# Both mixtures of experts by rows sorted on the chip, in phases, in place of every expert on every row

## The reference

```python
x = L0_attn_x                                  # (16, 256, 128) f32
xn = layernorm(x)
s = L0_attn(xn)                                # linear attention, 16 heads of 64
h = xn + small_causal_attention(rmsnorm(xn))   # 16 heads of 8
h2 = rmsnorm(h)
topw, topi = top_k(softmax(h2 @ gate_w.T), 2)  # weights made to sum to 1
for e in range(8):                             # F = 256
    g = silu(h2 @ w1[e].T) * (h2 @ w3[e].T)
    out += (g @ w2[e].T) * wfull[:, e:e + 1]   # 0 but for the two chosen
x = x + s * silu(h + out)
xn = layernorm(x)
s = L1_attn(xn)                                # chunked gated linear attention, then an FFN of 512
top1 = argmax(xn @ Wg + bg)
y = relu(xn @ W1[e] + b1[e]) @ W2[e] + b2[e]   # H = 512, all e; the chosen one is kept
x = x + s * silu(y[top1])
```

## Time and profile before

| | |
|---|---|
| median of 3 runs | 2884.62 us |
| the profiled execution: its time, its span | 2885.05 us, 2883.3 us |
| busy: TensorE, VectorE, ScalarE, GpSimd | 2600.4, 1507.1, 1542.9, 77.0 us |
| TensorE's mean granted clock | 0.932 of full speed |
| moved by DMA | 85.37 MB, 30 GB/s on the mean |

### The profile page before, as it was taken

How to read it: one execution, slowest core, us unless ns; L and a number is a source line. 1 busy time by engine, 2 the same in 40 slices (tenths; PEclk the granted TensorE clock), 3 DMA queues, 4 the chain that set the end, 5 groups by cost and what they waited for, 6 DMA issues and landing times.

```text
span 2883.3 us, 54394 instructions
## 1 busy us (share of the span) xinstructions
PE 2600.4 (90%) x21120; PEld 1952.1 (68%) x21120; DVE 1507.1 (52%) x3781; ACT 1542.9 (54%) x2721; POOL 77.0 (3%) x40
## 2 busy tenths in 40 slices
PE   4789998999989899998998999899998999999987
PEld 3457767676776767757676676767766677676757
DVE  4355645455554555545455554656546456554543
ACT  1536475463745637375464745637466373744753
POOL 0000000000000000000000000000000000000000
PEclk9789989999999999989999998999989999998998
DMA  3000000100000000000100001000000000001011
GB/s 148 1 32 1 30 34 17 48 1 30 34 31 34 9 23 34 31 33 9 48 9 31 34 24 41 2 30 34 31 34 9 25 32 31 34 16 46 1 61 33
DMA packets 31411, 85.37 MB, mean 30 GB/s; under 512 B 4127, under 2 KB 13351, under 8 KB 30632
## 3 DMA queue, kind: packets, MB, share of 16 engines
q1 hardware_dynamic: 31144, 81.64, 8.2%
HBM read 79.53 MB, written 2.10 MB: 28 GB/s over the span
## 4 chain that ended last, share of the span: by engine, by line
PE 72%; DVE 10%; ACT 8%; issue 8%; SPq 1%; DVEq 0%; DMA 0%; ACTq 0%
PE psum L488 7%; PE psum L495 7%; PE psum L690 4%; PE psum L550 4%; PE psum L468 3%; PE psum L650 3%; PE psum L794 3%; PE psum L520 3%; PE psum L637 2%; PE psum L538 2%; PE psum L741 2%; PE psum L621 2%; PE psum L475 2%; PE psum L577 2%; PE psum L558 2%
## 5 line engine op out<-in xcount | busy, mean ns | idle before, releaser
L894 ACT ACTIVATE gbuf<-psum,cols 128x256 f32<-128x256 f32 x512 | 201.8, 473 | 598.4 <-PE psum L495 582.2
L488 PE MATMUL psum<-x1T_s,ew 128*128 128x256 f32 x1024 | 270.2, 413 | 21.5 <-issue 21.5
L495 PEld LDWEIGHTS psum<-ew,gbuf 128*128 128x128 f32 x2048 | 254.2, 197 | 15.8 <-ACT gbuf L894 9.2
L495 PE MATMUL psum<-ew,gbuf 128*128 128x128 f32 x2048 | 257.2, 280 | 4.1 <-ACT gbuf L894 4.1
L488 PEld LDWEIGHTS psum<-x1T_s,ew 128*128 128x128 f32 x1024 | 200.7, 205 | 87.2 <-issue 61.3
L1156 DVE SCALAR_TENSOR_TENSOR acc<-psum,small,acc 128x128 f32<-128x128 f32 x256 | 77.9, 346 | 335.4 <-PE psum L495 335.4
L468 PE MATMUL psum<-hT_s,w13T 128*128 128x256 f32 x1024 | 243.4, 384 | 0.0
L468 PEld LDWEIGHTS psum<-hT_s,w13T 128*128 128x128 f32 x1024 | 191.6, 192 | 43.7 <-issue 22.1
L880 ACT ACT_TABLE_LOAD x144 | 184.8, 1283 | 2.5
L876 ACT ACT_TABLE_LOAD x128 | 164.2, 1283 | 2.2 <-PE psum L468 0.6
L1131 DVE TENSOR_TENSOR gbuf<-gbuf,psum 128x512 f32<-128x512 f32 x128 | 87.7, 685 | 145.1 <-ACT gbuf L876 145.1
(11 more groups left out here) (212 smaller groups left out, 4828.6 us busy)
## 6 DMA issues: line engine op xcount, KB each, us to landing
ew<-in_ew SPq DMA_DIRECT2D x128, 512.0 KB, 3.6
x<-in_x SPq DMA_DIRECT2D x16, 128.0 KB, 2.1
w13T<-in_w13T SPq DMA_DIRECT2D x1, 2048.0 KB
lqkvg<-in_lqkvg SPq DMA_DIRECT2D x1, 2048.0 KB
out<-y SPq DMA_DIRECT2D x16, 128.0 KB, 1.9
wqkv<-in_wqkv SPq DMA_DIRECT2D x1, 1536.0 KB, 6.5
w2T<-in_w2T SPq DMA_DIRECT2D x1, 1024.0 KB
wrope<-in_wrope SPq DMA_DIRECT2D x1, 640.0 KB, 7.5
```

The costliest lines, as they stand in the source:

```text
L488: last = mm(bank(f"h{e}{j}")[:, a * N:(a + 1) * N], ew[:, e % EB, c * P:(c + 1) * P], x1T[:, :], start=True, stop=True)
L495: last = mm(bank(f"yy{e - 1}")[:, t * P:(t + 1) * P], r1[:, c, t * P:(t + 1) * P], ew[:, (e - 1) % EB, F1 + c * D:F1 + (c + 1) * D], start ...
L894: ins = af(r1[:, c, :], bank(f"h{e}{j}")[:, a * N:(a + 1) * N], ACT.Relu, bias=cols[:, 8 + 4 * e + c:9 + 4 * e + c])
```

## The change

The mixtures are computed for the chosen rows alone. A stage G or a part of C gives each token a slot in a region of its expert in memory (`rows0` and `rows1`, one for each half of 8 batch rows): the token's rank among the same expert's tokens comes from five small products with a triangle of ones (`rank`), a running count is kept in `cnt`. GpSimd scatters the rows there with an indirect DMA. After 8 batch rows VectorE makes a table on one partition (`table`, 14 small operations): for each of 40 tiles of 128 slots (24 are used by the second mixture) its place and its expert. SyncE reads place and expert into registers and loads a tile's weights (384 KB, or 578 KB) and its rows. `tile_step(u)` then does one tile in three steps, each a step behind the one before: transpose, hidden layer, output. SyncE stores a tile's output to `outs0` or `outs1`, and GpSimd gathers each token's two rows (or one) back by the slots, when the row's next stage begins.

As the rows of 8 batch rows must be there before any tile of theirs, the program runs in phases, and what a later stage needs of a row (attention, x2, weights, slots) goes to memory and back (`keepA`, `keepC`):

| segment | times | holds |
|---|---|---|
| H | 1 | the norm of row 0 |
| AH, AHG | 1, 8 | first attention, next row's norm; G: slots and scatter of the row before |
| AHGB | 6 | the same with 5 tiles of the first mixture (first half) |
| AGB, GB | 1, 1 | the last first attention, then tiles and slots alone |
| CB | 8 | second attention of the first half, 5 tiles of the first mixture (second half) |
| CD | 8 | second attention of the second half, 3 tiles of the second mixture (first half) |
| DE | 8 | 3 tiles (second half), outputs of the first half |
| E | 8 | outputs of the second half |

Silu and the last gate of the first mixture are built as Exp, Ln(1 + .), Exp (`logistic`), so that no table is loaded in A and B. The next row's norm (`head`) now stands at the end of the first attention, between `x2` and `h2` on VectorE; `norms1` at the start of the second, behind the gathers. The choice of the second mixture moves ahead of the chunk products' multiply on VectorE. Buffers `w13T`, `w2T` and `ew` go. In the first eight AHG bodies SyncE fills the four regions with zeros (33.5 MB).

```diff
-SEGMENTS = [("AB", 1), ("ABC", 1), ("ABCD", B - 2), ("CD", 1), ("D", 1)]
+HB = B // 2
+CAP = HB * N
+NTB, TB = 40, 5
+NTD, TD = 24, 3
+SEGMENTS = [("H", 1), ("AH", 1), ("AHG", HB), ("AHGB", HB - 2), ("AGB", 1), ("GB", 1), ("CB", HB), ("CD", HB), ("DE", HB), ("E", HB)]
...
+            def tile_loads(stage, count, weights, view):
...
+                for s in range(count):
+                    sp.wait_ge(*given(f"tile{s}_out"))
...
+                    where = sp.value_load(tab[0:1, which, bass.ds(j, 1)], min_val=0, max_val=ROWS // P - 1)
+                    expert = sp.value_load(tab[0:1, which, bass.ds(j + NTB, 1)], min_val=0, max_val=E - 1)
+                    places.append(where)
+                    sp.dma_start(view[:, s, :], weights[expert]).then_inc(sem(f"tile{s}_loaded"), 16)
+                    sp.dma_start(tx[:, s, :], XR[table].rearrange("(j p) d -> j p d", p=P)[where]).then_inc(sem(f"tile{s}_loaded"), 16)
...
+            def attention1():
+
+                g.wait_ge(*given("inA_free"))
...
+                g.dma_start(inA[:, :], KA[row("C")]).then_inc(sem("inA_ready"), 16)
+                g.dma_start(xC[:, :, :], A["x"][row("C")].rearrange("(t p) d -> p t d", p=P)).then_inc(sem("inA_ready"), 16)
+                g.wait_ge(*given("inA_ready", 1, 32))
...
+                        nc.gpsimd.indirect_dma_start(yg[:, k, t, :], None, YR[half("C")], bass.IndirectOffsetOnAxis(ap=slots_in[:, c:c + 1], axis=0)).then_inc(sem("yg_ready"), 16)
                 g.wait_ge(*given("cd_ready"))
...
+                g.wait_ge(*given("slots1_ready"))
...
+                    nc.gpsimd.indirect_dma_start(XR[half("C")], bass.IndirectOffsetOnAxis(ap=slotsC[:, t:t + 1], axis=0), xn1[:, t, :], None).then_inc(sem("scattered1"), 16)
+                g.wait_ge(*given("scattered1", 1, 32))
...
+            def tile_step(u):
...
+                if u < count:
+                    pe.wait_ge(*given(f"tile{u}_loaded", 1, 32))
+                    pe.wait_ge(*emptied(f"tx{u}"))
+                    tr(bank(f"tx{u}")[:, 0:P], tx[:, u, :]).then_inc(*fills(f"tx{u}"))
+                if 1 <= u <= count:
...
+                    for c in range(4):
+                        last = mm(bank(f"th{s}")[:, c * P:(c + 1) * P], view[:, s, c * P:(c + 1) * P], txT[:, s, :], start=True, stop=True)
+                    last.then_inc(*fills(f"th{s}"))
+                if 2 <= u <= count + 1:
...
+                    parts, hidden, w2 = (2, gB, wB) if "B" in stages else (4, rD, wD)
+                    for c in range(parts):
+                        last = mm(bank(f"ty{s}")[:, 0:D], hidden[:, s, c, :], w2[:, s, 4 * P + c * D:4 * P + (c + 1) * D], start=(c == 0), stop=(c == parts - 1))
...
+            def logistic(dst, src, ready):
+
+                af(dst, src, ACT.Exp, scale=-1.0).then_inc(*signals("act_chain"))
+                act.wait_ge(*chained("act_chain"))
+                af(dst, dst, ACT.Ln, bias=1.0).then_inc(*signals("act_chain"))
+                act.wait_ge(*chained("act_chain"))
+                af(dst, dst, ACT.Exp, scale=-1.0).then_inc(*signals(ready))
...
             def attention1():
-                moe0(0)
-                moe0(1)
...
+                dve.wait_ge(*given("yg_ready", 1, 64))
...
+                ins.then_inc(*signals("acc0_ready"))
...
+                v.tensor_tensor(x1[:, :, :], gated, xC[:, :, :], ALU.add).then_inc(*signals("inA_free"))
...
+                norms1()
+                z_inputs()
+                tile_step(0)
...
+            def outputs():
+
+                dve.wait_ge(*given("sgE_ready"))
+                v.tensor_tensor(sgE[:, :, :], sgE[:, :, :], y2_in, ALU.mult).then_inc(*signals("dve_chain"))
+                dve.wait_ge(*chained("dve_chain"))
+                dve.wait_ge(*given("stored", 1, 16))
+                v.tensor_tensor(ob[:, :, :], sgE[:, :, :], x1_in, ALU.add).then_inc(*signals("out_ready"))
```

More of the change, by code:

```diff
@@ L161 @@
+    "D": {**{f"{name}{s}_{what}": 1 for s in range(TD) for name, what in TILE_STEPS}},
+    "E": {"dve_chain": 1, "inC_free": 1, "inC_ready": 1, "out_ready": 1, "sgE_ready": 1, "stored": 1, "yd_ready": 1},
 }
@@ L295, in row, with half, all_given @@
             return now["i"] + rows_before(stage)
+        def half(stage):
+            return rows_before(stage) // HB
+        def all_given(name, by=1, first=0):
+            return sem(name), sum(times * in_body(stages, name) for stages, times in SEGMENTS[:now["n"] + 1]) * by + first
         def bank(use):
@@ new lines, in _ @@
+            for buffer in XR + YR:
+                sp.dma_start(buffer[E * CAP:].rearrange("(p r) d -> p (r d)", p=P), zero_rows[:, 0:8 * D]).then_inc(sem("later_zeros"), 16)
+            for s in range(TB):
+                sp.sem_inc(sem(f"tile{s}_stored"), 16)
+            sp.sem_inc(sem("recA_stored"), 16)
+            sp.sem_inc(sem("recC_stored"), 16)
+            def tile_loads(stage, count, weights, view):
+                table, which = half(stage), half(stage) + (0 if stage == "B" else 2)
+                places = []
+                for s in range(count):
+                    sp.wait_ge(*given(f"tile{s}_out"))
+                    sp.sem_inc(sem("tile_turn"), 1)
+                    j = now["i"] * count + (rows_before(stage) - half(stage) * HB) * count + s
+                    where = sp.value_load(tab[0:1, which, bass.ds(j, 1)], min_val=0, max_val=ROWS // P - 1)
[3 more added lines that the diff above has]
+                    sp.dma_start(tx[:, s, :], XR[table].rearrange("(j p) d -> j p d", p=P)[where]).then_inc(sem(f"tile{s}_loaded"), 16)
+                return places
@@ new lines, in tile_stores, with zero_fill @@
+            def tile_stores(stage, count, places):
+                table = half(stage)
+                for s in range(count):
+                    sp.wait_ge(*given(f"tile{s}_out", 2))
+                    sp.dma_start(YR[table].rearrange("(j p) d -> j p d", p=P)[places[s]], ty[:, s, :]).then_inc(sem(f"tile{s}_stored"), 16)
+            def zero_fill():
+                g = row("G")
+                for e in range(E):
+                    part = XR[0][e * CAP:(e + 1) * CAP].rearrange("(n p r) d -> n p (r d)", n=HB, p=P)
+                    sp.dma_start(part[g], zero_rows[:, 0:2 * D]).then_inc(sem("rows_zeroed"), 16)
+                for buffer in (XR[1], YR[0], YR[1]):
+                    part = buffer[0:E * CAP].rearrange("(n p r) d -> n p (r d)", n=HB, p=P)
+                    sp.dma_start(part[g], zero_rows).then_inc(sem("later_zeros"), 16)
@@ L415, in _ @@
                         body()
+                segment(n, 0)
+                after()
             sp.wait_ge(sem("stored"), 16 * (B + 1))
@@ L907, in norms1, with head @@
                 rstd("ln1b", small[:, 1:4:2], small[:, 4:6], 1.0, eps)
+            def head():
+                if "H" not in now["stages"]:
+                    return
+                rstd("ln0", small[:, 1:4:2], small[:, 4:6], 1.0, eps)
+                rstd("rms0", small[:, 6:8], small[:, 8:10], 1.0 / D, eps)
             def z_products(t):
```

881 lines of the change are left out of this document (516 added, 365 removed).

## The result

| | before | after |
|---|---|---|
| median (4 runs each) | 2883.44 us | 3029.89 us |
| ratio | | 1.0507, 95% interval 1.0485 to 1.0530 |
| the profiled execution: time, span | 2885.05, 2883.3 us | 3032.59, 3030.9 us |

What follows compares the result with a forecast made beforehand. The chain through ScalarE and VectorE, not TensorE's busy time, was taken to end a row after the change; 27 + 1323 + 18 + 1493 + 141 + 96 + 34 = 3132 us, taken as 3120 for overlap, range 2940 to 3320.

Steps and rivals of the forecast that it cites:

- 16 first attentions: Sum of bare bodies of 72.4 us with moved norm, loops and slots, seven carrying five tiles at +10: 1323 us.
- 16 second attentions: Bare 74.5 us, 10.2 between them, loop 2.8; first-mixture tiles +8.7, second-mixture tiles +4: 1493 us.
- DE: 8 short bodies of 3 second-mixture tiles with outputs: load, half-clock tile chain, output and loop, 17.6 us each, 141 us.
- E: Last 8 bodies, outputs alone: a load, two chained gathers, ScalarE and VectorE work, the loop; 12 us each, 96 us.
- The cover: Main loop: dense mixtures' matmuls fill TensorE's waits and half-clock time, making it only 27 us longer than both attentions bare.
- "+2.0" for the loops: First attentions: 14 looping bodies have no other work while engines wait for issue at the loop's return: +2.0 us each.
- "+2.0" for the slots: 14 first attentions: eight operations of 0.17 us with their gaps, where VectorE sets the pace: +2.0 us each.
- the loop's 2.8: Second attentions: VectorE's issue wait on return to the loop's top, added as 2.8 us a body.
- GpSimd's queue: Rival: scatter, record, row and gathers in each second attention at 6 us each become the bound: 3360 us, chance 0.12.
- Late tiles: Rival: tile loads from one queue at a body's start make tile 0 wait 5 us in 31 bodies: 3275 us, chance 0.10.
- Clock: Rival: TensorE's clock holds in both attentions, giving back at most 25 us a row, 400 in all: 2720 us, chance 0.08.
- the bound of 13.8 us a first attention: Bare first attention: full clock instead of half clock for 38% of 72.4 us would give back at most 13.8 us.

Runs made afterwards that it cites:

- warm_e: Kernel after plus 8 dummy products between the transposes of the negated maxima and 3 before the exponentials' products, in first attentions only; 2957.88 us, 1.0256 of before.
- warm_ac: Kernel after plus dummy products ahead of TensorE's waits in both attentions, nothing left out; 2847.94 us, 0.9896 of the kernel before.
- warm_c: Kernel after plus dummy products ahead of TensorE's waits in the second attention alone; 2919.22 us, 1.0107 of the kernel before.
- warm_pipe: Kernel after plus dummy products in both attentions, 12 more between two rows' states, and output phases written out row by row; 2793.98 us, 0.9667 of before.
- no_tiles: Kernel after with the tile steps of both mixtures left out; 2785.64 us, 0.9653 of the kernel before.

## Why the prediction was right, and where not

3120 us forecast, 3029.89 measured, slower as forecast and within 2940 to 3320. The slowdown itself was put at 8% and is 5.1%; the errors of the terms leave 101 us, and the attentions alone are 114 too high. Two small slips of addition are in the sum: the pieces ahead of a second attention make 9.8 us, not 10.2, and those of its first-mixture tiles 8.5, not 8.7, about 8 us in all. The sum of 3132 against the span of 3030.9, term by term:

| term | forecast | measured |
|---|---|---|
| start to the first product | 27 | 32.6 |
| 16 first attentions | 1323 | 1256 |
| a body of tiles alone | 18 | 14 |
| 16 second attentions | 1493 | 1446 |
| DE | 141 | 164 |
| E | 96 | 79 |
| phases and the rest | 34 | 39 |

**The cover** was right, and shown twice: by the loop of the kernel before with two experts (15.9 of 43 us), and by the bodies without tiles.

**The first attentions are 67 us too high.** The step that failed is "+2.0" for the loops and "+2.0" for the slots: bare 78.8 forecast, 75.1 measured. The first row's body, with the moved norm but no loop and no slots, takes 74.57 against 72.36, so the norm cost 2.2 of its 2.4; loop and slots together then cost 0.5. The idle issue at a loop's return seems to be no cost of its own where TensorE would wait for VectorE's operation L1557 at the same point; no run separates the two. Five tiles cost 7.5 instead of 10: I had added their VectorE time to the clock's, and the tiles in fact raise the clock.

**The second attentions are 47 too high.** Bare 83.6 to 84.2 against 87.5: probably again the loop's 2.8, which I took as additive. First-mixture tiles cost 9.6 (8.7 forecast), second ones 3.3 (2.9).

**DE is 23 too low**, the mis-sized term. By its timeline: 2.4 us from the output store to the first load, 4.2 to land, 2.9 until the second tile's rows are there, 9.1 of products, 1.7 to the output. I had forgotten that the first tile's hidden layer stands behind the second tile's transpose in the order of the steps, and had priced a register load at 0.5 us where two of them with their wait take 1.6 (2.49 us from one tile's load to the next, of which two issues are 0.9). **E is 17 too high**: 3.75 us from the record's issue to the first gather's, where I had 3.2; 3.84 from there to ScalarE (2982.32 to 2986.16), where I had 4.2; 2.25 until the next record is issued; the last is output and loop together, which I had at 1.9 + 2.8.

**The start** gained 4.5 us instead of 10. **Phases**: a change costs 13.8 us between CB and CD (107.6 against 93.8 from body to body), 2.8 more than forecast; of the change after GB, VectorE's table is 4.4 us and the rest is the record and the gathers, nothing behind them.

**The rivals.** *GpSimd's queue*: refuted; an issue is 0.96 us, and the gathers hold VectorE up in 3 of 16 rows. The Trainium skill (SBUF — State Buffer, Who interferes with whom) speaks of an issue from GpSimd that is held up while VectorE is in a two-port mode; the 64 scatters of the first attentions take 956 to 1127 ns with a median of 962, so no run here shows it as a cost. No trace tells whether VectorE was in such a mode beside them. *Late tiles*: no wait of TensorE for a tile's rows in the attention bodies; the 88.8 us in 17 waits are all in DE. *Clock*: it fell to 0.81, as the forecast had it, and the bound of 13.8 us a first attention was sound: 10.2 is there to be had. What I did not see is that the bound was also a price list. I treated the clock as something that happens to a kernel, and gave 0.08 to its holding; dummies in fourteen places take most of it back. The Trainium skill (TensorE: Matmul & The Clock Gate, HAM oscillation — how this bites in real kernels) describes an engine that falls back in every iteration because a DMA wait stands between two bursts, and advises a restructuring. Here the trace of after shows such a fall-back in all 16 rows behind a wait for VectorE (`mneg`) of at most 2.5 us; in warm_e it has gone from all 16, and a bare body is 4.2 us shorter.

TensorE was busy 74%, against the 65% I had named as a sign: at half clock the same products are busy longer, so this sign was badly chosen. Of the other signs, the clock, the bare first attention (75.1) and the second with first-mixture tiles (93.8) lay within; the loaded first attention at 82.6 lay under 85, the second with second-mixture tiles at 86.9 just under 87, and the short bodies at 20.5 and 9.9 were not the 17 and 12.

What stays open: why the clock fell in warm_ac at a place where the same dummies held it in warm_c, and the bound of a DE body without its serial loads.

## What to carry to other kernels

When a change takes work off the busiest engine, measure the bare chain first: here the bare chain was 84% of the loop (146.9 of 174.1 us), so at the clock of that chain 57 us of matmuls a row could give back no more than 27, and the frame that a sparse version needs (memory round trips, phases, output bodies without cover) cost more. Where the profile shows TensorE's products behind a wait at twice their length, cheap dummy products ahead of that very wait returned the time here, and too many of them cost time (42 against 33 ahead of one wait: 4.1 us a body). Before a sparse and a dense version are compared, give both the same remedies: here they were equal with dummies, and the sparse one was ahead only once its output bodies were pipelined.

## What the runs showed of the hardware

- A wait of 2.45 us, with one product behind it and 0.94 us more of waiting, was followed by 14 us of products at 1.2 GHz; with dummies, the 0.67 us of idleness left there was followed by none.
- Whether the clock falls at a given place can differ from row to row with the same instructions: in warm_pipe the body from 563.7 us takes 68.0 us and runs at half clock from 610 to 618 us, behind waits of only 0.67, 0.42 and 0.76 us, where other rows take 64.9. That is also where the wider spread of these kernels' times may come from; it was not tested.
- An indirect DMA of 128 rows holds GpSimd 0.96 us, with 0.30 us between two, and the engine that waits for the rows goes on 1.6 us after the last issue ends (two gathers in an E body), or 2.8 us (four at a change of phase).
- Writing 4.2 MB of zeros in a body costs nothing that shows: a first attention takes 75.1 us on the mean with it (after, eight AHG bodies) and 75.1 in the six rows of no_tiles from 704.96 to 1155.62 us, which go on without it.
